# Attention with its weighing in two halves of 256 queries, and its projections in halves of 256 tokens

## The chip, the cores and the metric

The kernel runs on one core of a Trainium2 chip. The core has five engines with queues of their own: TensorE (matrix products, PE in the profile, with PEld for the loading of its weights), VectorE (DVE), ScalarE (ACT), GpSimd (POOL) and SyncE (SP, which issues DMAs here). They meet through semaphores only. The metric is the device time of one execution in microseconds (us); the time of a kernel is the median of its runs.

## The reference

Two layers, each with a norm ahead and behind and a residual: a state-space layer in two directions, and a transformer layer with attention and a mixture of experts. The change touches the attention alone, for 2 sequences of 2048 tokens and 16 heads of 16:

```python
q = (src @ q_w).reshape(b, s, h, hd).transpose(0, 2, 1, 3)
k = (src @ k_w).reshape(b, s, h, hd).transpose(0, 2, 1, 3)
v = (src @ v_w).reshape(b, s, h, hd).transpose(0, 2, 1, 3)
scores = jnp.einsum('bhqd,bhkd->bhqk', q, k) / np.float32(np.sqrt(hd))
scale = jax.nn.sigmoid(jnp.einsum('bhsd,hd->bhs', q, scale_w)) * 2.0
scores = scores * scale[..., None]
aw = jax.nn.softmax(scores, axis=-1)
out = jnp.einsum('bhqk,bhkd->bhqd', aw, v).transpose(0, 2, 1, 3).reshape(b, s, d)
```

## The kernel before

The program has three parts, one behind the other: the state-space layer (to about 670 us), the attention (670 to 2257 us), then gate, routing and experts. The attention works on groups of 4 heads of one sequence (8 groups, `GROUPS`), each in 4 units of 512 queries (`UNITS`, 32 in all), each unit in 16 tiles of 128 keys (`KT`). One tile of a unit is a step here; there are 512.

**A step.** For each of its four heads a step does four things. Two engines share a maximum: TensorE multiplies 128 queries with 512 keys ("max", L1574) and VectorE takes the largest of each row (L1666). This runs `LEAD` = 20 steps ahead of the rest, since a unit's maxima must be complete, negated and put into the query stack before its scores. TensorE multiplies 128 keys with the unit's 512 queries ("score", L1559), the maximum's rows included, so that the difference comes out at once. ScalarE takes the exponential, two heads in one instruction (L1630). TensorE then weighs the values with them ("weigh", L1605) and adds up over the 16 tiles in one PSUM bank, `pv`: the four heads' 17 columns (16 values and a column of ones for the sum) stand side by side in four column groups of the array and run at the same time. The weighing is fp32, so the one matmul of the program is two on the chip, which makes 8 for four heads.

Scores and maxima use 50 and 48 rows of the array: the even heads have the lower half of its rows, the odd heads the upper. A max of an even head and a score of an odd one can run at the same time.

**The order.** `attention_order` writes one list of steps, and each engine does its own part of it in that order. In step t stand max 0, score 1, score 0, max 1, max 2, score 3, score 2, max 3, then the weighing of step t - 1, then what a table `due` plans for this step. The waits that matter here: a max waits until the bank that it writes is free (three banks, `rbank`, in turn, each freed by a reduce or by another reader); score 1 waits for the exp of heads 0 and 1 of the step before, score 3 for that of heads 2 and 3, since they overwrite what it reads; the weighing of a step waits for its two exps; an exp waits for the weighing two steps back, whose input it overwrites.

**What `due` plans.** Once a unit: `negate` (the maxima's sign and split), `turn_rows` (four transposes that make rows of the maxima, a ScalarE copy, DMAs into the query stack) and `turn_out` (four transposes of the weighed sum; the copies L1646 and L1649 and the division around it). Once a group, for the group after it, two batches of `SPLIT`: two projections of 512 tokens to queries and keys (L1081: two matmuls over the depth, four on the chip, then a ScalarE copy, L1101), `scale` (L1091, a Tanh), `multiply` and `high` (L1110, two casts) and `save` (DMAs by SyncE). `SPLIT_AT` gives the steps at which they stand, counted from the batch's first. All of them use the three banks too.

**The first stage.** The first group's projections are in `residual_and_values`, with the residual and the values of the state-space layer's last tokens. The words of `STAGE3` set each engine's order there. Its projections and scales use two banks in turn.

## Time and profile before

| what | value |
|---|---|
| median of 3 runs | 2612.39 us (2609.77 to 2612.70) |
| the profiled execution | 2606.42 us |
| its span, first to last instruction | 2604.6 us |
| TensorE busy | 2455.2 us (94%) |
| VectorE busy | 2103.3 us (81%) |
| ScalarE busy | 1785.0 us (69%) |
| GpSimd busy | 940.3 us (36%) |
| mean granted TensorE clock | 0.972 |

The profile comes from one execution on the chip. A busy time counts an engine's own instructions, not its waits. Matmuls are pipelined, so one that waits for its turn can count as busy: TensorE's 94% does not say that it has no slack. A timeline row merges equal instructions that follow each other (x4): its length then runs from the first one's start to the last one's end. Two rows of TensorE may overlap where they use different halves or columns of the array. The brackets at a row's end give the engine's idle time before it and what ended it. For what a step costs, the distance from one start to the next says more than the lengths. A granted clock of 1.00 is 2.4 GHz, one of 0.50 is 1.2 GHz.

### The profile page before, as it was taken

The numbers are of one execution on the slowest core, as the hardware profiler recorded it, in microseconds if no ns is written. First come the engines' busy times: TensorE is split into PE (matmuls) and PEld (weight loads), VectorE is DVE, ScalarE is ACT, GpSimd is POOL, SyncE is SP. The second block draws the span as 40 slices with busy tenths as digits, with TensorE's granted clock in tenths as the row PEclk, the third lists the DMA queues.
The fourth block names the chain that finished last, engine by engine and source line by source line (L and its number), as shares of the span: only waits on it lengthen the run. The fifth ranks groups of instructions, "written<-read, shape, count | busy, mean of one in ns | idle before, by whom it ended". The sixth has DMA issues, their size and how long they took to land. (4 is left out here: it accounts for less than half of the span.)

```text
span 2604.6 us, 41005 instructions
## 1 busy us (share of the span) xinstructions
PE 2455.2 (94%) x14283; PEld 1173.9 (45%) x14283; DVE 2103.3 (81%) x4155; ACT 1785.0 (69%) x2336; POOL 940.3 (36%) x1059
## 2 busy tenths in 40 slices
PE   7899999999799999999999999999999999897996
PEld 5566655555443333333333333333333333374654
DVE  6778888998768888888888888898899988184886
ACT  4888877777216777777777777777777777862664
POOL 1787888888600112111121121111111010146664
PEclk8999999999878999999999999999999999997998
DMA  3322332232420403104031040040040000125883
GB/s 106 121 82 82 104 95 89 94 108 78 113 55 17 66 18 54 29 18 50 17 47 20 18 63 3 18 66 10 8 66 2 1 2 1 52 90 184 295 288 108
DMA packets 96431, 178.17 MB, mean 68 GB/s; under 512 B 19382, under 2 KB 66150, under 8 KB 88400
## 3 DMA queue, kind: packets, MB, share of 16 engines
q1 hardware_dynamic: 89488, 160.43, 24.4%
q0 software_dynamic: 6016, 14.49, 1.6%
q8 instruction: 114, 1.87, 0.3%
q14 instruction: 93, 0.76, 0.1%
q10 hardware_dynamic: 720, 0.62, 0.1%
HBM read 145.11 MB, written 31.21 MB: 68 GB/s over the span
## 5 line engine op out<-in xcount | busy, mean ns | idle before, releaser
L1666 DVE TENSOR_REDUCE max_part<-round_psum 128x1 f32<-128x512 f32 x2048 | 1271.5, 683 | 220.6 <-PE round_psum L1574 217.4
L1630 ACT ACTIVATE p_exp<-score_psum 128x1024 f32<-128x1024 f32 x1024 | 991.8, 1022 | 287.5 <-PE score_psum L1559 280.0
L1574 PE MATMUL round_psum<-k_stack,q_stack 48*128 48x512 f32 x2048 | 781.2, 459 | 45.7 <-DVE max_part L1666 12.3
L1574 PEld LDWEIGHTS round_psum<-k_stack,q_stack 48*128 48x128 f32 x2048 | 342.4, 186 | 714.0 <-DVE max_part L1666 599.3
L1559 PE MATMUL score_psum<-q_stack,k_stack 50*128 50x512 f32 x2048 | 634.6, 428 | 3.2 <-ACT p_exp L1630 3.2
L1605 PE MATMUL pv_psum<-p_exp,values 128*17 128x512 f32 x4096 | 540.4, 599 | 0.0
L1559 PEld LDWEIGHTS score_psum<-q_stack,k_stack 50*128 50x128 f32 x2048 | 326.2, 185 | 27.3 <-ACT p_exp L1630 23.5
L672 PE MATMUL rot<-tokens_t,w_in 128*128 128x512 f32 x576 | 271.3, 602 | 0.5 <-DVE x_conv L839 0.2
L1709 POOL TENSOR_TENSOR rden<-pv_out,minus_one 128x16 f32<-128x16 f32 x31 | 90.0, 2902 | 439.8 <-ACT pv_out L1649 437.2
L1696 POOL CAST max_parts<-max_neg 128x16 fp32r<-128x16 f32 x32 | 6.4, 199 | 471.6 <-DVE max_neg L1672 451.0
L672 PEld LDWEIGHTS rot<-tokens_t,w_in 128*128 128x128 f32 x576 | 104.3, 193 | 97.5 <-issue 88.1
L930 POOL TENSOR_TENSOR decay<-cum_rows_in,scan_cum 128x1024 f32<-128x1024 f32 x64 | 121.4, 1898 | 55.5 <-DMA cum_rows_in<-cum_rows 34.9
L831 DVE SCALAR_TENSOR_TENSOR rot<-conv_in,chan,rot 128x512 f32<-128x512 f32 x160 | 120.4, 752 | 18.2 <-ACT rot L753 14.6
L723 PE MATMUL rows_psum<-w_out,y_gated 128*128 128x256 f32 x512 | 127.8, 393 | 0.0
L1605 PEld LDWEIGHTS pv_psum<-p_exp,values 128*17 128x17 f32 x4096 | 68.1, 95 | 126.3 <-issue 117.1
L1118 POOL TENSOR_SCALAR split_then_gate<-split_then_gate 128x512 f32<-128x512 f32 x16 | 9.9, 621 | 269.6 <-ACT split_then_gate L1106 269.6
L723 PEld LDWEIGHTS rows_psum<-w_out,y_gated 128*128 128x128 f32 x512 | 93.5, 193 | 10.3
L787 ACT ACTIVATE decay<-decay 128x1024 f32<-128x1024 f32 x64 | 67.4, 1053 | 25.1 <-POOL decay L930 25.1
L1129 POOL TENSOR_TENSOR split_then_gate<-split_then_gate 128x512 f32<-128x512 f32 x32 | 40.3, 1283 | 119.7 <-ACT split_then_gate L1110 119.7
L936 POOL TENSOR_TENSOR c_decayed<-c_decayed,c_t 128x512 f32<-128x512 f32 x60 | 76.8, 1279 | 16.6 <-ACT c_t L772 15.0
L863 DVE TENSOR_TENSOR decay<-decay,gb_psum 128x1024 f32<-128x1024 f32 x64 | 77.9, 1217 | 4.8 <-ACT decay L789 2.2
L693 PE MATMUL y_psum<-decay,x_dt 128*64 128x128 f32 x1024 | 70.9, 281 | 11.3 <-DVE decay L863 8.3
(296 smaller groups left out, 3317.9 us busy)
## 6 DMA issues: line engine op xcount, KB each, us to landing
cum_rows_in<-cum_rows SPq DMA_DIRECT2D x64, 512.0 KB, 3.9
expert_w<-in_expert_w SPq DMA_DIRECT2D x24, 1028.0 KB
qk_rows<-split_then_gate SPq DMA_DIRECT2D x64, 256.0 KB, 4.0
tokens_t<-in_expert_w SPq DMA_DIRECT2D x15, 1028.0 KB, 7.8
cum_pairs_in<-cum_rows SPq DMA_DIRECT2D x240, 64.0 KB, 2.8
q_stack<-qk_rows SPq DMA_DIRECT2D x42, 256.0 KB, 11.7
k_stack<-qk_rows SPq DMA_DIRECT2D x42, 256.0 KB, 15.0
token_rows<-tokens SPq DMA_DIRECT2D x12, 512.0 KB, 4.0
```

Of the source, the lines that this page charges most:

```text
L672: m = nc.tensor.matmul(bank[n, c][:, :], w_in[:, k, col:col + P], xnT[:, k, span(block_at(n) * BLK, BLK, d)], start=(k == 0), stop=(k == K ...
L723: m = nc.tensor.matmul(rows_bank[:, 0:D], yg[:, two, c, :], w_out[d][:, c, :], start=False, stop=(c == CI - 1), skip_group_check=True)
L831: nc.vector.scalar_tensor_tensor(t[:, :], pre[:, c, i:i + BLK], tap(d, c, i), t[:, :], ALU.mult, ALU.add).then_inc(*own.up())
L863: nc.vector.tensor_tensor(mm, mm, over_mid(masked, NH), ALU.mult).then_inc(*m_ready.up(q))
L930: nc.gpsimd.tensor_tensor(heads(M[:, two, :], NH, P), heads(cum[:, q % 2, :], NH, P), over_last(scan_of("cum", d, q), P), ALU.subtract).th ...
L936: nc.gpsimd.tensor_tensor(ceh, ceh, over_mid(CT[:, sl, ch], NH // 2), ALU.mult).then_inc(*c_ready.up(q))
L1559: m = nc.tensor.matmul(ebank[i // 2][:, i % 2, :], ks[rows, n % 2, plane, k * P:(k + 1) * P], qs[rows, n % 2, plane, q * BLK:(q + 1) * BLK ...
L1574: nc.tensor.matmul(bank[step][:, :], qs[rows, n % 2, plane, at:at + P], ks[rows, n % 2, plane, keys * BLK:(keys + 1) * BLK], start=True, s ...
L1605: m = nc.tensor.matmul(pv[h * 32:h * 32 + VW, :], V[:, b * KT + k, g * HG + h, :], pt[:, (k * 2 + h // 2) % 4, h % 2, :], start=(k == 0), ...
L1630: nc.scalar.activation(pt[:, (k * 2 + pair) % 4, :, :], ebank[pair][:, :, :], ACT.Exp).then_inc(*exped.up(u, k, pair))
L1666: nc.vector.tensor_reduce(mx[:, c * HG + h, keys:keys + 1], bank[step][:, :], AX_X, ALU.max).then_inc(*maxed.up(u, k, i))
L1709: nc.gpsimd.tensor_tensor(rden[:, :], o[:, :, HD], minus[:, :].to_broadcast([P, CPB * HG]), ALU.pow).then_inc(*denominator.up(u))
```

## The change

The weighing of a step is cut into two halves of 256 queries each. The first half of step t - 1 stands behind score 3 of step t, the second half behind score 1 of step t + 1, so that two maxima's products lie between one half and the next. All eight matmuls become sixteen on the chip, with the same weights loaded for both halves. Both halves write the same bank; only the first clears it. The exps wait for the second half, and so does the copy of a unit's weighed sum, which now stands one step later on TensorE and is wanted by the next unit's first half in the same step.

The projections of 512 tokens are cut in two as well (256 tokens, half a bank, a copy of half the length each). In the main part they stand at the batch's steps 0, 2, 4 and 6 where they stood at 0 and 4; scale, multiply, high and save keep their steps. In the first stage the second batch's last two quarters stand behind `turn4`, since their banks come free with copies that ScalarE does behind `turn4`.

```diff
-SPLIT = (("project", 0), ("project", 1), ("scale", 0), ("multiply", 0), ("high", 0), ("save", 0))
-SPLIT_AT = (0, 4, 8, 10, 14, 18)
+SPLIT = (("project", 0), ("project", 1), ("project", 2), ("project", 3), ("scale", 0), ("multiply", 0), ("high", 0), ("save", 0))
+SPLIT_AT = (0, 2, 4, 6, 8, 10, 14, 18)
+PART = BLK // 2
...
-        s = 2 * j + i
-        cols = slice(b * SEQ + s * BLK, b * SEQ + (s + 1) * BLK)
+        s, half = 2 * j + i // 2, i % 2
+        first = b * SEQ + s * BLK + half * PART
+        cols = slice(first, first + PART)
...
-            m = nc.tensor.matmul(bank[:, :], S.w_qk[:, k, g, i * w:(i + 2) * w], S.srcT[:, k, cols], start=(k == 0),
-                                 stop=(k == KD - 1))
-        m.then_inc(*S.projected.up(n, s))
+            m = nc.tensor.matmul(bank[:, 0:PART], S.w_qk[:, k, g, i // 2 * w:(i // 2 + 2) * w], S.srcT[:, k, cols],
+                                 start=(k == 0), stop=(k == KD - 1))
+        m.then_inc(*S.projected.up(n, s, half))
...
-        nc.scalar.copy(S.parts[:, i, 1, :], bank[:, :]).then_inc(*S.raw_in.up(n, s))
+        nc.scalar.copy(S.parts[:, i // 2, 1, half * PART:(half + 1) * PART],
+                       bank[:, 0:PART]).then_inc(*S.raw_in.up(n, s, half))
...
-    "PE": "project00 project01 scale0 project10 project11 values0 values1 turn4 scale1 values2 values3 turn5 "
+    "PE": "project00 project01 project02 project03 scale0 project10 project11 values0 values1 turn4 project12 project13 "
+          "scale1 values2 values3 turn5 "
...
-        if weighing:
-            yield "weigh", *divmod(t - 1, KT), 0
+            if left == ("max", 0) and 0 <= t - 2 < total:
+                yield "weigh", *divmod(t - 2, KT), 1
+            if left == ("max", 2) and 0 <= t - 1 < total:
+                yield "weigh", *divmod(t - 1, KT), 0
...
-                    if k == 0 and u:
+                    if k == 0 and i == 0 and u:
                         pe.wait_ge(*pv_out.at(u - 1))
+                    part = slice(i * PART, (i + 1) * PART)
                     for h in range(HG):
-                        if h % 2 == 0:
+                        if h % 2 == 0 and i == 0:
                             pe.wait_ge(*exped.at(u, k, h // 2))
-                        m = nc.tensor.matmul(pv[h * 32:h * 32 + VW, :], V[:, b * KT + k, g * HG + h, :],
-                                             pt[:, (k * 2 + h // 2) % 4, h % 2, :], start=(k == 0), stop=(k == KT - 1),
-                                             skip_group_check=True)
-                        if h % 2:
+                        m = nc.tensor.matmul(pv[h * 32:h * 32 + VW, part], V[:, b * KT + k, g * HG + h, :],
+                                             pt[:, (k * 2 + h // 2) % 4, h % 2, part], start=(k == 0 and i == 0),
+                                             stop=(k == KT - 1), skip_group_check=True)
+                        if h % 2 and i:
                             m.then_inc(*weighed.up(u, k, h // 2))
...
-                if what == "weigh" and k == KT - 1:
+                if what == "weigh" and k == KT - 1 and i:
```

In the order of TensorE a plain step stood like this before (L1574 a max, L1559 a score, L1605 the weighing of four heads; "x2" are two instructions in a row; the first row is a step's first max):

```order
L1574 MATMUL round_psum1<-k_stack,q_stack 128x512
L1559 MATMUL score_psum0<-q_stack,k_stack 128x512 x2
L1574 MATMUL round_psum2<-k_stack,q_stack 128x512
L1574 MATMUL round_psum0<-k_stack,q_stack 128x512
L1559 MATMUL score_psum1<-q_stack,k_stack 128x512 x2
L1574 MATMUL round_psum1<-k_stack,q_stack 128x512
L1605 MATMUL pv_psum<-p_exp,values 17x512 x4
```

And like this now (L1581 a max, L1566 a score, L1613 half a weighing), again from a step's first max to the next step's:

```order
L1581 MATMUL round_psum0<-k_stack,q_stack 128x512
L1566 MATMUL score_psum0<-q_stack,k_stack 128x512
L1613 MATMUL pv_psum<-p_exp,values 17x256 x4
L1566 MATMUL score_psum0<-q_stack,k_stack 128x512
L1581 MATMUL round_psum1<-k_stack,q_stack 128x512
L1581 MATMUL round_psum2<-k_stack,q_stack 128x512
L1566 MATMUL score_psum1<-q_stack,k_stack 128x512
L1613 MATMUL pv_psum<-p_exp,values 17x256 x4
L1566 MATMUL score_psum1<-q_stack,k_stack 128x512
L1581 MATMUL round_psum0<-k_stack,q_stack 128x512
L1581 MATMUL round_psum1<-k_stack,q_stack 128x512
```

The weighing of 512 queries at the step's end is gone; half of one stands between score 1 and score 0, which write the same bank pair, and half of one between score 3 and score 2.

A projection stood between a weighing and the next step's first max on TensorE (L1081; the row says x2 for the depth's two halves):

```order
L1574 MATMUL round_psum1<-k_stack,q_stack 128x512
L1605 MATMUL pv_psum<-p_exp,values 17x512 x4
L1081 MATMUL round_psum2<-tokens_t,split_then_gate 128x512 x2
L1574 MATMUL round_psum0<-k_stack,q_stack 128x512
L1559 MATMUL score_psum0<-q_stack,k_stack 128x512 x2
```

Now a half of one (L1084) stands between a step's last max and the next step's first:

```order
L1613 MATMUL pv_psum<-p_exp,values 17x256 x4
L1566 MATMUL score_psum1<-q_stack,k_stack 128x512
L1581 MATMUL round_psum2<-k_stack,q_stack 128x512
L1084 MATMUL round_psum0<-tokens_t,split_then_gate 128x256 x2
L1581 MATMUL round_psum1<-k_stack,q_stack 128x512
L1566 MATMUL score_psum0<-q_stack,k_stack 128x512
```

It is no longer behind a weighing, it writes 256 columns instead of 512, and there are twice as many such places.

ScalarE's copies of the projections (L1101 before, L1104 now) lie between the exps (L1630, L1638). Before, at one batch:

```order
L1101 COPY split_then_gate<-round_psum 128x512
L1630 ACTIVATE p_exp<-score_psum 128x1024 x8
L1101 COPY split_then_gate<-round_psum 128x512
L1641 COPY max_rows<-round_psum 8x512
L1630 ACTIVATE p_exp<-score_psum 128x1024 x6
L1646 COPY pv_out<-pv_psum 128x512
L1630 ACTIVATE p_exp<-score_psum 128x1024 x2
```

And now, the end of the same batch:

```order
L1638 ACTIVATE p_exp<-score_psum 128x1024 x4
L1104 COPY split_then_gate<-round_psum 128x256
L1649 COPY max_rows<-round_psum 8x512
L1638 ACTIVATE p_exp<-score_psum 128x1024 x4
L1104 COPY split_then_gate<-round_psum 128x256
L1638 ACTIVATE p_exp<-score_psum 128x1024 x2
L1654 COPY pv_out<-pv_psum 128x512
L1638 ACTIVATE p_exp<-score_psum 128x1024 x2
```

The copy of the weighed sum (L1646, now L1654) keeps its place among the exps; the projections' copies are half as long, and four exps apart instead of eight.

## Rows read from the trace of the kernel before

**Rows 1.** Busy time by window: each engine's us (x instructions), clock, DMA share, GB/s.
```profile
770.00:795.00 25.00, 23.93 (x65) 11.86 (x65) 16.62 (x28) 7.20 (x11) 2.92 (x4) 0.50 0.17 44
795.00:2200.00 1405.00, 1368.18 (x8161) 513.09 (x8157) 1211.33 (x1971) 1027.46 (x1126) 204.83 (x275) 1.00 0.17 27
```

**Rows 2.** Groups by line, 795 to 2212 us: count | busy us, mean ns | idle before, releaser.
```profile
L1666 DVE TENSOR_REDUCE max_part<-round_psum 128x1 f32<-128x512 f32 x1959 | 1216.3, 683 | 195.1 <-PE round_psum L1574 192.1
L1630 ACT ACTIVATE p_exp<-score_psum 128x1024 f32<-128x1024 f32 x980 | 949.9, 1022 | 280.7 <-PE score_psum L1559 273.2
...
L1605 PE MATMUL pv_psum<-p_exp,values 128*17 128x512 f32 x3920 | 515.8, 598 | 0.0
...
L1081 PE MATMUL round_psum<-tokens_t,split_then_gate 128*128 128x512 f32 x104 | 51.6, 618 | 0.0
...
L1614 PE MATMUL round_psum<-const_f,pv_out 128*128 128x128 f32 x120 | 19.7, 287 | 0.0
L1593 PE MATMUL round_psum<-const_f,max_parts 128*8 128x128 f32 x120 | 18.0, 273 | 0.0
L1646 ACT COPY pv_out<-pv_psum 128x512 f32<-128x512 f32 x30 | 17.6, 588 | 4.2 <-PE pv_psum L1605 0.3
...
L1110 ACT CAST split_then_gate<-split_then_gate 128x512 fp32r<-128x512 f32 x26 | 14.8, 627 | 0.0
```

**Rows 3.** Timeline of one plain step: start us, length us, instruction, [idle before <-releaser].
```profile
2021.70 0.50 PE L1574 MATMUL round_psum<-k_stack,q_stack 48*128 48x512 f32 x1
...
2022.04 0.39 PE L1574 MATMUL round_psum<-k_stack,q_stack 48*128 48x512 f32 x1
...
2022.24 2.48 DVE L1666 TENSOR_REDUCE max_part<-round_psum 128x1 f32<-128x512 f32 x4 [0.22 <-PE round_psum L1574]
2022.28 0.40 PE L1574 MATMUL round_psum<-k_stack,q_stack 48*128 48x512 f32 x1
2022.47 1.94 ACT L1630 ACTIVATE p_exp<-score_psum 128x1024 f32<-128x1024 f32 x2 [0.77 <-PE score_psum L1559]
...
2022.98 0.18 PEld L1574 LDWEIGHTS round_psum<-k_stack,q_stack 48*128 48x128 f32 x1 [0.52 <-DVE max_part L1666]
2022.98 0.50 PE L1574 MATMUL round_psum<-k_stack,q_stack 48*128 48x512 f32 x1
...
2023.41 1.05 PE L1605 MATMUL pv_psum<-p_exp,values 128*17 128x512 f32 x8
...
2024.39 0.49 PE L1574 MATMUL round_psum<-k_stack,q_stack 48*128 48x512 f32 x1
...
2024.39 0.73 PE L1559 MATMUL score_psum<-q_stack,k_stack 50*128 50x512 f32 x2
```

**Rows 4.** Timeline, TensorE: four matmuls of 256 columns, and four of 512 (a projection).
```profile
756.26 1.13 PE L1585 MATMUL score_psum<-w_v,tokens_t 128*128 128x256 f32 x4
757.33 0.50 PE L1574 MATMUL round_psum<-k_stack,q_stack 48*128 48x512 f32 x2
...
900.28 1.98 PE L1081 MATMUL round_psum<-tokens_t,split_then_gate 128*128 128x512 f32 x4
...
902.20 0.50 PE L1574 MATMUL round_psum<-k_stack,q_stack 48*128 48x512 f32 x1
```

**Rows 5.** Timeline of the last steps, which have no maxima.
```profile
2212.39 0.73 PE L1559 MATMUL score_psum<-q_stack,k_stack 50*128 50x512 f32 x4
...
2212.94 3.77 ACT L1630 ACTIVATE p_exp<-score_psum 128x1024 f32<-128x1024 f32 x4 [0.53 <-PE score_psum L1559]
...
2214.93 0.19 PEld L1559 LDWEIGHTS score_psum<-q_stack,k_stack 50*128 50x128 f32 x2 [0.70 <-ACT p_exp L1630]
...
2251.78 0.92 PE L1559 MATMUL score_psum<-q_stack,k_stack 50*128 50x512 f32 x4
```

**Rows 6.** Timeline, TensorE, from the first stage's last turns to the first max.
```profile
712.72 1.80 PE L1295 MATMUL score_psum<-const_f,p_exp 128*128 128x128 f32 x8 [0.61 <-DVE p_exp L1337]
...
717.43 1.19 PE L1574 MATMUL round_psum<-k_stack,q_stack 48*128 48x512 f32 x3 [2.91 <-DMA k_stack<-qk_rows]
```

More of the change, by code:

```diff
@@ L1046, in __init__ @@
         self.filled = sems.dma("rows_fill", self.fills)
-        self.projected = sems.events("qk_projected", blocks)
+        parts = [(n, s, half) for n, s in blocks for half in range(2)]
+        self.projected = sems.events("qk_projected", parts)
         self.scaled = sems.events("qk_scale_summed", halves)
-        self.raw_in = sems.events("qk_raw_stored", blocks)
+        self.raw_in = sems.events("qk_raw_stored", parts)
         self.ez_in = sems.events("qk_scale_exp", halves)
@@ L1073, in split_on_tensor @@
     if what == "project":
-        s = 2 * j + i
-        cols = slice(b * SEQ + s * BLK, b * SEQ + (s + 1) * BLK)
-        if (n, s) in ((0, 0), (1, 0)):
+        s, half = 2 * j + i // 2, i % 2
+        first = b * SEQ + s * BLK + half * PART
+        cols = slice(first, first + PART)
+        if (n, s, half) in ((0, 0, 0), (1, 0, 0)):
             pe.wait_ge(*S.loaded[n].at(0))
@@ L1089, in split_on_tensor @@
         for s, x, _, q in S.blocks(j):
-            pe.wait_ge(*S.raw_in.at(n, s))
+            pe.wait_ge(*S.raw_in.at(n, s, 1))
             m = nc.tensor.matmul(bank[q, :], S.w_sc[q, g, :], x[q, :], start=True, stop=True, skip_group_check=True)
@@ L1096, in split_on_scalar @@
     if what == "project":
-        s = 2 * j + i
-        act.wait_ge(*S.projected.at(n, s))
-        if (n, j) != (0, 0):
+        s, half = 2 * j + i // 2, i % 2
+        act.wait_ge(*S.projected.at(n, s, half))
+        if (n, j) != (0, 0) and half == 0:
             act.wait_ge(*(S.saved[s - 2].at(n, "k") if j else S.saved[s + 2].at(n - 1, "k")))
-        nc.scalar.copy(S.parts[:, i, 1, :], bank[:, :]).then_inc(*S.raw_in.up(n, s))
+        nc.scalar.copy(S.parts[:, i // 2, 1, half * PART:(half + 1) * PART],
+                       bank[:, 0:PART]).then_inc(*S.raw_in.up(n, s, half))
     if what == "scale":
@@ L1165 @@
     "SP": "weights0 load4 load7 weights1 load6 load5 keep4 keep5 save0 fill stack0 keep6 save1 keep7",
-    "PE": "project00 project01 scale0 project10 project11 values0 values1 turn4 scale1 values2 values3 turn5 "
+    "PE": "project00 project01 project02 project03 scale0 project10 project11 values0 values1 turn4 project12 project13 "
+          "scale1 values2 values3 turn5 "
           "turn6 turn7",
-    "ACT": "project00 project01 scale0 high0 values0 values1 turn4 project10 project11 scale1 values2 high1 "
+    "ACT": "project00 project01 project02 project03 scale0 high0 values0 values1 turn4 project10 project11 project12 project13 scale1 values2 high1 "
            "turn5 turn6 turn7 values3",
@@ L1219, in bank_read @@
         what, n, j, i = u
-        return S.raw_in.at(n, 2 * j + i) if what == "project" else S.ez_in.at(n, j)
+        return S.raw_in.at(n, 2 * j + i // 2, i % 2) if what == "project" else S.ez_in.at(n, j)
     x_load = [sems.dma(f"x_again{b}", [b]) for b in later]
@@ L1418, in attention_order @@
     for t in range(-LEAD, total + 4):
-        scoring, weighing, ahead = 0 <= t < total, 0 < t <= total, 0 <= t + LEAD < total
+        scoring, ahead = 0 <= t < total, 0 <= t + LEAD < total
         u, k = divmod(t, KT)
@@ L1505, in bank_read @@
             return out_in.at(n)
-        return S.raw_in.at(n, 2 * j + i) if what == "project" else S.ez_in.at(n, j)
+        return S.raw_in.at(n, 2 * j + i // 2, i % 2) if what == "project" else S.ez_in.at(n, j)
     def back(u, k, n):
@@ L1543, in _ @@
             pe.wait_ge(*zero.at(0))
-            pe.wait_ge(*S.raw_in.at(0, SB - 1))
+            pe.wait_ge(*S.raw_in.at(0, SB - 1, 1))
             pe.wait_ge(*S.ez_in.at(0, 1))
```

## The prediction

> **What bounds the kernel now.** I read the windows first: from 795 to 2200 us, more than half of the span, TensorE is busy 1368 of 1405 us at the full granted clock of 1.00 (2.4 GHz), VectorE 1211, ScalarE 1027 [rows 1]. All of the change's main part lies there. Then the groups of lines, for the size of one of each [rows 2], and one plain step in order of time [rows 3]. A step is one tile of 128 keys for one unit: four maxima's products ("max", L1574), four score products (L1559), two exps, one weighing (L1605).
>
> In [rows 3] the step runs from the max at 2021.70 to the next one's at 2024.39: 2.69 us. The reader is to see one closed circle in it. The first max starts at 2021.70; VectorE begins to reduce it at 2022.24 (0.54 later); the fourth max needs the bank that this reduce gives back and starts at 2022.98 (0.74 later, its weights' load idle for 0.52 "<-DVE max_part"); the weighing starts 0.43 later, and the next step's first max 0.98 after that. 0.54 + 0.74 + 0.43 + 0.98 = 2.69. VectorE itself needs only 2.40: four reduces take 2.48 from first start to last end, one is 0.68 long, so one starts every 0.60. ScalarE needs 1.84: two exps take 1.94, one 1.02, so one starts every 0.92. So neither TensorE's work nor VectorE's is the limit, but their turn-taking: four maxima come in a bunch, then none while TensorE weighs.
>
> **The weighing in halves.** Three prices from [rows 3], counted from start to start. A product that finds its weights loaded ahead takes 0.40, one that stands first after another shape of work 0.50. From such a first pair to the next pair it is 0.34 (2021.70 to 2022.04), later 0.24. A weighing starts 0.07 before the last product ends (2022.98 + 0.50 against 2023.41), so 0.43 after the start of a first one and 0.33 after the start of one with its weights ahead.
>
> The trace has no weighing of 256 queries. A full one holds TensorE 0.98. What 256 columns less are worth is read from the projections [rows 4]: four matmuls of 512 columns hold it 1.92 (900.28 to 902.20), four of 256 columns 1.07 (756.26 to 757.33), so 0.2125 for one. The weighing's four heads run side by side, in two rounds: 490 weighings of 8 matmuls are busy 515.8 us, 1.05 each, though one matmul lasts 0.598 [rows 2]. A half then holds TensorE 0.98 - 2 x 0.2125 = 0.555. Below, everything could halve: 0.49. Above, by the group of 256 columns, which loads 128 weight columns instead of 17, two of its four matmuls less: 1.07 - 0.425 = 0.645. I take 0.555, which comes from the weighing's own row; the ends go into the range.
>
> The new step has three bounds.
> TensorE's own work: first pair and half a weighing behind it (0.43 + 0.555), first pair again and a pair with weights ahead (0.34 + 0.33), second half (0.555), first pair (0.34): 2.55.
> VectorE: 2.40. The fourth max now comes 2.21 after the first, its bank is free after 1.28, so the wait of today is gone.
> A new circle through ScalarE: score 1 waits for the exp of the step before (that wait stands today too, with 0.9 us to spare: the exp that starts at 2022.47 is over at 2023.49 and the score starts at 2024.39). From now on half a weighing stands between score 1 and score 0, and score 0 is what the next exp wants. Score 1 to half weighing 0.43, half weighing 0.555, score 0 and up to the exp's start 0.50 + 0.04 (2022.04 + 0.40 to 2022.47), exp 1.02, and 0.05 from its end to the next score 1: in [rows 5] the second exp of the row at 2212.94 starts 0.92 later and ends at 2214.88, and the weights' load that waited for it starts at 2214.93. Sum 2.595. Queued behind that waiting score are the half weighing, the next maxima and all else of TensorE.
> The longest is the new circle: **2.595 against 2.69**, 0.095 less a step. That is what the change gains, a third of what VectorE alone would allow. There are 492 steps with maxima: 492 x 0.095 = **-46.7 us**.
>
> **The steps without maxima.** The last 20 steps have none. Today they go at ScalarE's pace: from 2212.39 to 2251.78 are 19 steps, 2.07 each [rows 5]. The new circle has no max in it, so it holds there too: 20 x (2.595 - 2.07) = **+10.5**.
>
> **The projections.** Counts of the main part from [rows 2]: 104 matmuls are 26 projections, at 1.92 more each: 49.9 us. They become 52. One stands between the last pair (which then costs 0.43 instead of 0.34) and the next step, and takes 1.07: the step is 2.55 + 0.09 + 1.07 = 3.71, 1.115 above 2.595; together 58.0, **+8.1**. The ScalarE copies are half as long and fit beside; a bank is held for a shorter time. SyncE's and GpSimd's queues keep their steps: scale, multiply, high and save stand at the same steps as before.
>
> **Other work that meets the new circle.** 30 turns of the maxima's rows and 30 of the output (120 matmuls in fours of each kind): today each adds its own length, in future its length + 0.09 - 0.045 (2.595 is 0.045 above TensorE's 2.55): 60 x 0.045 = **+2.7**. 13 pairs of casts (L1110, 26 of 0.627): two hold ScalarE about 1.05. The second exp starts 1.225 after the first (0.34 + 0.33 + 0.555) and is on for 0.92, so ScalarE has 2.595 - 1.225 - 0.92 = 0.45 free before the next first exp: 0.60 late each time. Today the free stretch is 0.77 (2022.47 in [rows 3]), 0.28 late: 13 x 0.32 = **+4.2**. The 30 copies of the weighed sum (L1646, 0.588, some 0.49 to the next start): 0.04 over the free 0.45, and the next unit's first half weighing now waits for them within the same step: 0.05 each, **+1.5**.
>
> **The start.** Two of the first batch's quarter projections move behind turn 4 on TensorE, and the scale, the values and the last turns are queued behind them, at a clock that is low in places (0.50 from 770 to 795, [rows 1]): 2 to 4 us later. TensorE is 2.9 us idle before the first max, which waits for k_stack's DMA at 717.43, and is done with the turns at 714.5 [rows 6]. That hides most: **+1** (0 to 2).
>
> **Sum:** -46.7 + 10.5 + 8.1 + 2.7 + 4.2 + 1.5 + 1 = **-18.7 us**. The profiled execution took 2606.42 (span 2604.6 and 1.8 around it): 2587.7. The median of the three runs is 6.0 above it; the same step off 2612.39 gives **2594 us**.
>
> **Rivals.** Faster still: a half weighing is nearer to 0.49. The circle is then 2.53 and TensorE 2.42: 492 x 0.16 = 78.7 off, the others as above (+17.5) with 9.2 instead of 10.5 for the last steps: -52, **2560**. For it: the weighing's weights are 17 columns wide, little to load. Against: each change of shape costs the same drain however short the work.
>
> Slower: the half weighing is not nearly half. At 0.645 TensorE itself is the bound, 2.55 + 0.18 = 2.73: 492 x 0.04 = +20, last steps +12.3 (the circle is 2.685), projections 58.5 + 1 - 49.9 = +9.6, turns 60 x 0.09 = +5.4, the rest +6.7: **+54, 2666**. It decides from where the step's gain no longer pays the 28 us of the other terms: 28 / 492 = 0.057, a step of 2.633, a half weighing of 0.59. For it: the one group of 256 columns that the trace has lies above that. Against: its weights are the wide ones.
> The Trainium skill speaks for this one ("TensorEngine Tiling (Array Packing)", section "Instruction Overhead"): each matmul has about 60 cycles of overhead on TRN2. The step gets eight matmuls more; at 2.4 GHz that is, as an estimate, 0.2 us a step and a half weighing of 0.655, about as in this rival. The trace speaks against it so far: eight matmuls of 0.598 within 1.05 [rows 2] do not queue for their overhead one by one.
>
> No change: the gain is there, but ScalarE's small works do not fit into its free stretches, which are now two, of 0.3 and 0.45, where there was one. If the 30 copies of the weighed sum fall on the circle in full, 0.49 each instead of 0.05, it is +13.2: **2607**, and a half weighing 0.01 longer makes it 2612. For it: ScalarE is in the circle, as it isn't today. Against: the copies stand where the longer stretch is.
>
> **How the numbers follow.** The forecast (half weighing 0.51 to 0.58): 0.50. Faster still: 0.14. No change: 0.18. Slower: 0.18. What a measurement of this kernel can tell from no change is about 0.2%, 5 us. The forecast's and the faster rival's chances make faster 0.64. The range leaves out the deeper half of the fast rival and the deeper half of the slow one: a half weighing of 0.51 (circle 2.55) gives -41, one of 0.60 (TensorE 2.64) +7: 2572 to 2620. TensorE's clock in the lead (0.50 in [rows 1]) may fall at other places, some us either way, within it.
>
> **What would show it.** In the profile after: a plain step of 2.58 to 2.61; ahead of score 1 an idle stretch that ends with an exp, and none any more that ends with a reduce ahead of the fourth max; a half weighing that holds TensorE 0.55; VectorE and ScalarE with more busy share there; the last 20 steps near 2.6 instead of 2.07; a quarter projection at 1.07. If the plain step is 2.69 or more with TensorE never idle, the half weighing was mis-sized; if it is under 2.55, the circle through ScalarE was.

## The result and the profile after

The changed kernel takes 2596.88 us (median of 15 runs, 2583.94 to 2611.38), the kernel before 2611.74 (median of 15 runs beside it). The ratio is 0.9942, with a 95% interval of 0.9924 to 0.996: 14.9 us faster, 0.6%. Predicted were 2594 and 18.7 us less. The profiled executions differ by 16.4 us: a span of 2588.2 after, 2604.6 before. Of all executions below, one of adjacent's ten took 3029.64 us at a mean granted clock of 0.721; it counts in adjacent's median, but in no ratio.

Where these 16.4 us lie is read from the starts of the first max, of the first exp, of the first exp of step 491 (the last one with maxima) and of step 511 (the last one):

| stretch | before, us | after, us | difference | predicted |
|---|---|---|---|---|
| up to the first max | 717.4 | 717.2 | -0.2 | +1 |
| first max to first exp (the lead) | 70.9 | 67.8 | -3.2 | 0, some us either way |
| first exp to step 491 | 1422.1 | 1392.3 | -29.8 | -30.2 |
| the last 20 steps | 41.9 | 53.2 | +11.4 | +10.5 |
| the rest (last turn, gate, experts) | 352.3 | 357.7 | +5.4 | 0 |
| span | 2604.6 | 2588.2 | -16.4 | -18.7 |

The -30.2 are the prediction's steps, projections, turns, casts and copies together. The two stretches that the change touches in earnest came out within 1 us of the prediction each. The lead, with two of the projections in it, and the rest, which the change doesn't touch, are taken up in the last section.

The windows of the kernel after that answer to [rows 1] (time, then each engine's busy time and instructions, the granted clock, DMA share, GB/s):

```profile
770.00:795.00 25.00, 24.29 (x99) 11.16 (x98) 18.01 (x31) 9.56 (x13) 2.49 (x2) 0.57 0.16 43
795.00:2176.00 1381.00, 1376.30 (x12196) 599.46 (x12192) 1242.53 (x1981) 1079.07 (x1157) 204.82 (x275) 1.00 0.17 28
```

In the main part TensorE leaves 4.7 us free where it left 37. VectorE's share is 90.0% (86.2% before), ScalarE's 78.1% (73.1%): the same work in less time. TensorE looks like the bound. That it isn't can't be read from this sum, but from the order within one step and from an experiment, both below: by the profile's own note the matmuls' ends are modelled, and a wait of some 0.05 us ahead of one hardly shows in such a sum.

The groups by line of the kernel after, 795 to 2178 us, for [rows 2] (count | busy us, mean ns | idle before, releaser):

```profile
L1674 DVE TENSOR_REDUCE max_part<-round_psum 128x1 f32<-128x512 f32 x1954 | 1239.1, 687 | 137.6 <-PE round_psum L1581 109.1
L1638 ACT ACTIVATE p_exp<-score_psum 128x1024 f32<-128x1024 f32 x977 | 999.7, 1025 | 295.2 <-PE score_psum L1566 295.2
...
L1613 PE MATMUL pv_psum<-p_exp,values 128*17 128x256 f32 x7812 | 611.6, 385 | 1.9
...
L1581 PEld LDWEIGHTS round_psum<-k_stack,q_stack 48*128 48x128 f32 x1953 | 296.6, 184 | 39.8 <-DVE max_part L1674 30.1 <-issue 9.4 <-ACT pv_out L1657 0.2
...
L1084 PE MATMUL round_psum<-tokens_t,split_then_gate 128*128 128x256 f32 x208 | 58.8, 405 | 0.0
```

And of the kernel before, the group that loads the weights of the maxima's products, 795 to 2212 us:

```profile
L1574 PEld LDWEIGHTS round_psum<-k_stack,q_stack 48*128 48x128 f32 x1957 | 325.2, 184 | 679.6 <-DVE max_part L1666 576.0 <-issue 28.5 <-ACT pv_out L1649 13.4
```

The wait that the change was to remove is gone: the idle time of these loads that ends with a reduce fell from 576.0 us to 30.1, and none of what is left stands ahead of a fourth max. The 576.0 are not all that wait, though. By the max that a load is for, 230.6 of them stand ahead of a fourth max (490 loads, 0.52 in [rows 3]) and 345.5 ahead of a step's first (426 loads), most of these behind a weighing, like this one:

```profile
2024.39 0.18 PEld L1574 LDWEIGHTS round_psum<-k_stack,q_stack 48*128 48x128 f32 x1 [0.85 <-DVE max_part L1666]
```

There only the loading of weights is idle; TensorE is busy with the weighing (2023.41 to 2024.46, [rows 3]) and loses nothing by it. So the change could gain far less than these 576 us; the steps with maxima became 29.8 us shorter. The weighing's matmuls are twice as many (7812) and their busy time grew from 515.8 to 611.6.

One plain step of the kernel after, in order of time (start, length, instruction, [idle before and what ended it]), for [rows 3]:

```profile
2034.24 0.50 PE L1566 MATMUL score_psum<-q_stack,k_stack 50*128 50x512 f32 x1
...
2034.66 0.63 PE L1613 MATMUL pv_psum<-p_exp,values 128*17 128x256 f32 x8
...
2035.22 0.49 PE L1566 MATMUL score_psum<-q_stack,k_stack 50*128 50x512 f32 x1
...
2035.56 0.40 PE L1566 MATMUL score_psum<-q_stack,k_stack 50*128 50x512 f32 x1
2035.75 1.02 ACT L1638 ACTIVATE p_exp<-score_psum 128x1024 f32<-128x1024 f32 x1 [0.34 <-PE score_psum L1566]
...
2035.89 0.63 PE L1613 MATMUL pv_psum<-p_exp,values 128*17 128x256 f32 x8
...
2036.44 0.50 PE L1566 MATMUL score_psum<-q_stack,k_stack 50*128 50x512 f32 x1
...
2036.83 0.50 PE L1566 MATMUL score_psum<-q_stack,k_stack 50*128 50x512 f32 x1
```

This is the new circle. Score 1 starts at 2034.24, the half weighing 0.42 later, score 0 another 0.56 later (2035.22), the exp that wants score 0 at 2035.75 (0.53); the exp lasts 1.02, to 2036.77; the next step's score 1 starts 0.06 after that, at 2036.83. 0.42 + 0.56 + 0.53 + 1.02 + 0.06 = 2.59. The step is 2.59 long.

The last steps of the kernel after, which have no maxima, for [rows 5]:

```profile
2179.36 0.74 PE L1566 MATMUL score_psum<-q_stack,k_stack 50*128 50x512 f32 x2
...
2179.89 1.02 ACT L1638 ACTIVATE p_exp<-score_psum 128x1024 f32<-128x1024 f32 x1 [0.34 <-PE score_psum L1566]
...
2180.97 0.18 PEld L1566 LDWEIGHTS score_psum<-q_stack,k_stack 50*128 50x128 f32 x1 [0.21 <-ACT p_exp L1638]
...
2182.49 1.02 ACT L1638 ACTIVATE p_exp<-score_psum 128x1024 f32<-128x1024 f32 x1 [0.35 <-PE score_psum L1566]
```

From exp to exp it is 2182.49 - 2179.89 = 2.60, as in the steps with maxima, and not 2.07 as before. Here, where no max stands beside it, the profile names the wait: the weights' load of score 1 sat idle until the exp ended (2179.89 + 1.02 = 2180.91, load at 2180.97). This is the clearest single line for the circle.

### The profile page after: what moved, and what is told of

Read it like the earlier page. It is cut to its first block and busy times, and to the rows that moved or that the text cites. A ratio compares the mean times of both kernels' runs of the same rounds, so it can differ in the third digit from the quotient of the medians.

```text
span 2588.2 us, 49485 instructions
## 1 busy us (share of the span) xinstructions
PE 2467.5 (95%) x18507; PEld 1267.0 (49%) x18507; DVE 2129.0 (82%) x4155; ACT 1836.0 (71%) x2368; POOL 940.4 (36%) x1059
## 5 line engine op out<-in xcount | busy, mean ns | idle before, releaser
L1674 DVE TENSOR_REDUCE max_part<-round_psum 128x1 f32<-128x512 f32 x2048 | 1297.8, 687 | 161.6 <-PE round_psum L1581 132.8
L1638 ACT ACTIVATE p_exp<-score_psum 128x1024 f32<-128x1024 f32 x1024 | 1047.3, 1025 | 313.3 <-PE score_psum L1566 313.3
L1566 PE MATMUL score_psum<-q_stack,k_stack 50*128 50x512 f32 x2048 | 843.5, 474 | 4.7 <-ACT p_exp L1638 2.8
L1581 PE MATMUL round_psum<-k_stack,q_stack 48*128 48x512 f32 x2048 | 787.3, 461 | 8.5 <-DVE max_part L1674 4.9
L1613 PE MATMUL pv_psum<-p_exp,values 128*17 128x256 f32 x8192 | 642.3, 385 | 2.3 <-ACT pv_out L1654 0.3
L1566 PEld LDWEIGHTS score_psum<-q_stack,k_stack 50*128 50x128 f32 x2048 | 363.5, 184 | 478.8 <-issue 434.0
L1581 PEld LDWEIGHTS round_psum<-k_stack,q_stack 48*128 48x128 f32 x2048 | 313.9, 187 | 71.2 <-DVE max_part L1674 52.6
L1613 PEld LDWEIGHTS pv_psum<-p_exp,values 128*17 128x17 f32 x8192 | 136.0, 95 | 271.5 <-issue 257.5
L1084 PE MATMUL round_psum<-tokens_t,split_then_gate 128*128 128x256 f32 x256 | 75.2, 422 | 7.0 <-DMA split_then_gate<-in_w_qk 6.0
```

Of the source, the lines that this page charges most:

```text
L1566: m = nc.tensor.matmul(ebank[i // 2][:, i % 2, :], ks[rows, n % 2, plane, k * P:(k + 1) * P], qs[rows, n % 2, plane, q * BLK:(q + 1) * BLK ...
L1581: nc.tensor.matmul(bank[step][:, :], qs[rows, n % 2, plane, at:at + P], ks[rows, n % 2, plane, keys * BLK:(keys + 1) * BLK], start=True, s ...
L1613: m = nc.tensor.matmul(pv[h * 32:h * 32 + VW, part], V[:, b * KT + k, g * HG + h, :], pt[:, (k * 2 + h // 2) % 4, h % 2, part], start=(k = ...
L1638: nc.scalar.activation(pt[:, (k * 2 + pair) % 4, :, :], ebank[pair][:, :, :], ACT.Exp).then_inc(*exped.up(u, k, pair))
L1674: nc.vector.tensor_reduce(mx[:, c * HG + h, keys:keys + 1], bank[step][:, :], AX_X, ALU.max).then_inc(*maxed.up(u, k, i))
```

## The experiments

Two theories of the changed kernel's step stand against each other. By the first, the step is the circle through ScalarE, and cutting a weighing costs next to nothing. By the second, TensorE is the bound: it is busy 1376.30 of 1381 us, since eight more matmuls a step cost it what the removed wait gave. All seven runs, beside the two of above; the ratio is against runs of the kernel before beside them (medians 2610.15 for adjacent, weigh_only, project_only and short_exp, 2609.97 for the last three). "Plain step" is the median of the steps with nothing else in them:

| kernel | median, us | ratio (95%) | plain step | first exp to step 491 | last 20 steps |
|---|---|---|---|---|---|
| before | 2611.74 | | 2.69 | 1422.1 | 41.9 |
| changed | 2596.88 | 0.9942 (0.9924 to 0.996) | 2.59 | 1392.3 | 53.2 |
| adjacent | 2614.62 | 1.0015 (1.0005 to 1.0024) | 2.69 | 1424.6 | 41.9 |
| weigh_only | 2591.23 | 0.9931 (0.9913 to 0.9948) | 2.59 | 1388.4 | 53.2 |
| project_only | 2615.45 | 1.0025 (1.001 to 1.0039) | 2.69 | 1426.0 | 41.8 |
| short_exp | 2527.91 | 0.9677 (0.9662 to 0.9693) | 2.44 | 1341.5 | 45.6 |
| pairs_apart | 2515.71 | 0.9635 (0.9621 to 0.9649) | 2.44 | 1324.6 | 44.5 |
| pairs_apart_h | 2521.87 | 0.9656 (0.962 to 0.9692) | 2.44 | 1324.8 | 44.5 |
| changed_again | 2598.91 | 0.9949 (0.9929 to 0.997) | 2.59 | 1393.1 | 53.2 |

**adjacent: what does the cut itself cost?** The kernel before, with the weighing cut into the change's two halves, but both left where the whole one stood.

```
         if weighing:
             yield "weigh", *divmod(t - 1, KT), 0
+            yield "weigh", *divmod(t - 1, KT), 1
...
-                        m = nc.tensor.matmul(pv[h * 32:h * 32 + VW, :], V[:, b * KT + k, g * HG + h, :],
+                        m = nc.tensor.matmul(pv[h * 32:h * 32 + VW, part], V[:, b * KT + k, g * HG + h, :],
...
```

> The kernel before with each weighing cut into its two halves of 256 queries, but both halves left where the whole one stood, at the step's end, one behind the other; projections whole. It prices the cut alone. Theory (a half holds TensorE 0.555 because the change of shape ahead and behind is the fixed part, and the cut itself costs next to nothing): two halves side by side pay one change of shape, so they hold 0.98 to 1.01; a plain step of 2.69 to 2.72, 2612 to 2627 us. Rival (each set of matmuls has its own fixed part of 0.13): the two hold 1.11, a plain step of 2.82, 492 x 0.13 = 64 more, about 2676 us.

Measured: 2614.62, ratio 1.0015. The timeline of one step, TensorE:

```profile
2030.36 0.49 PE L1576 MATMUL round_psum<-k_stack,q_stack 48*128 48x512 f32 x1
...
2031.63 0.18 PEld L1576 LDWEIGHTS round_psum<-k_stack,q_stack 48*128 48x128 f32 x1 [0.52 <-DVE max_part L1669]
...
2032.06 1.06 PE L1608 MATMUL pv_psum<-p_exp,values 128*17 128x256 f32 x16
...
2033.05 0.49 PE L1576 MATMUL round_psum<-k_stack,q_stack 48*128 48x512 f32 x1
```

The 16 matmuls of both halves hold TensorE 2033.05 - 2032.06 = 0.99, where 8 of twice the length held it 0.98 [rows 3]; the step is 2.69 as before, with the old wait for a reduce (0.52) in it. So the eight matmuls more cost 0.01 us a step: the price of more matmuls, on which the slower rival and the second theory lean, isn't there. Whether halves that stand apart fill TensorE all the same, short_exp decides. The Trainium skill ("TensorEngine Tiling (Array Packing)", section "Instruction Overhead") gives each matmul an overhead of about 60 cycles; for eight that would be, as an estimate, 0.2 us. Four heads side by side on 32 columns each do not pay it one after the other here. The section can also be read as a least length (it says that one column takes as long as 60); a matmul of 256 columns would then pay nothing more, and the 0.01 agrees with that.

What a half costs when it stands apart is a second thing: 0.56 twice is 1.12, against 0.98. This 0.14 is what it costs that other products stand between the halves, one more change of shape, and it is in the prediction's 0.555.

**weigh_only and project_only: each half of the change alone.** The first has the halves of the weighing where the change puts them, and whole projections; the second the other way round.

```
# weigh_only, against the changed kernel
-SPLIT_AT = (0, 2, 4, 6, 8, 10, 14, 18)
+SPLIT_AT = (0, 4, 8, 10, 14, 18)
...
-            m = nc.tensor.matmul(bank[:, 0:PART], S.w_qk[:, k, g, i // 2 * w:(i // 2 + 2) * w], S.srcT[:, k, cols],
-                                 start=(k == 0), stop=(k == KD - 1))
+            m = nc.tensor.matmul(bank[:, :], S.w_qk[:, k, g, i * w:(i + 2) * w], S.srcT[:, k, cols], start=(k == 0),
+                                 stop=(k == KD - 1))
...
```

```
# project_only, against the changed kernel
-            if left == ("max", 0) and 0 <= t - 2 < total:
-                yield "weigh", *divmod(t - 2, KT), 1
-            if left == ("max", 2) and 0 <= t - 1 < total:
-                yield "weigh", *divmod(t - 1, KT), 0
+        if weighing:
+            yield "weigh", *divmod(t - 1, KT), 0
...
```

> The change without its second part: the weighing's halves two maxima's products apart, the projections whole as before. Theory: plain steps of 2.59 as in the changed kernel, last steps 2.6; a whole projection makes a step of 2.55 + 0.09 + 1.92 = 4.56, 1.97 over a plain one, 26 x 1.97 = 51 against 58 for 52 halves: 7 us less than the changed kernel, near 2590. Rival (halves of projections pay because VectorE and ScalarE run on meanwhile): 5 us or more above the changed kernel, 2602 or more.

> The change without its first part: whole weighings at the step's end as before, projections in halves, in the first stage too. Theory: plain steps of 2.69; a half projection adds 1.07 where a whole one adds 1.92, 52 x 1.07 - 26 x 1.92 = 5.7 more, about 2617 us. Rival (the halves of the projections carry part of the change's gain): 2607 or less.

Measured: 2591.23 and 2615.45. The weighing brings the whole gain. The projections' cut costs 3.9 us from the first exp to step 491 on either footing: 1392.3 against 1388.4 with the halves of the weighing, 1426.0 against 1422.1 without. In the median of the runs the cut alone is slower by little (ratio 1.0025, from 1.001 on). Between weigh_only and the changed kernel the medians differ by 5.7, but the intervals of their ratios overlap: the run times alone don't separate the two. (The cut has a second effect, in the lead; the last section has it.)

**short_exp: is it the circle through ScalarE?** The changed kernel, with each exp over 256 of its 512 columns a head; it leaves out the other 256, so the second half weighing reads what was left there.

```
-                    nc.scalar.activation(pt[:, (k * 2 + pair) % 4, :, :], ebank[pair][:, :, :],
+                    nc.scalar.activation(pt[:, (k * 2 + pair) % 4, :, 0:PART], ebank[pair][:, :, 0:PART],
```

> The changed kernel with each exp over half of its columns (two heads x 256 instead of 512), so the weighing's second half reads what was left there; TensorE's and VectorE's work is the same. It shortens only the circle score 1, half weighing, score 0, exp. Theory (that circle sets the 2.59): exp 0.59 instead of 1.02, circle 2.16, so TensorE is the bound with all weights loaded ahead, 0.33 + 0.555 + 0.34 + 0.33 + 0.555 + 0.34 = 2.45; plain steps of 2.45, 492 x 0.14 = 69 less, and about 8 less in the last 20 steps: near 2520 us. Rival (TensorE's own work is 2.59): plain steps stay at 2.59, only the last steps shorten, 2587 to 2597 us.

Measured: 2527.91, ratio 0.9677. One step:

```profile
1991.19 0.50 PE L1566 MATMUL score_psum<-q_stack,k_stack 50*128 50x512 f32 x1
...
1991.53 0.40 PE L1566 MATMUL score_psum<-q_stack,k_stack 50*128 50x512 f32 x1
...
1991.73 0.60 ACT L1638 ACTIVATE p_exp<-score_psum 128x512 f32<-128x512 f32 x1 [0.63 <-PE score_psum L1566]
1991.86 0.63 PE L1613 MATMUL pv_psum<-p_exp,values 128*17 128x256 f32 x8
...
1992.41 0.49 PE L1566 MATMUL score_psum<-q_stack,k_stack 50*128 50x512 f32 x1
...
1993.09 0.63 PE L1613 MATMUL pv_psum<-p_exp,values 128*17 128x256 f32 x8
...
1993.64 0.49 PE L1566 MATMUL score_psum<-q_stack,k_stack 50*128 50x512 f32 x1
```

TensorE has the same instructions as in the changed kernel, and the step falls from 2.59 to 1993.64 - 1991.19 = 2.45. An engine that is the bound doesn't get faster by another engine's shorter work, so TensorE wasn't: the circle was. 2.45 is then TensorE's own work, twice 0.34 + 0.33 + 0.555. The last 20 steps, too, lose 7.6 us. The whole is 8 us above what I expected: I had taken 0.14 off all 492 steps (69 us), and the steps with maxima lost 50.8 (1392.3 to 1341.5). The steps with a projection, a turn or a scale lost nothing (3.706 us with a projection in both), so TensorE held them already. The 340 plain ones lost 0.121 each on the mean (41 us), the 13 with casts 0.435 and the 23 with a copy of the weighed sum 0.165 (together 9.5). Their mean, 2.477, lies above their median of 2.45 since the first ones ran at a lower clock: from 784 to 800 us it was 0.50 on the mean, in the changed kernel 0.77.

**pairs_apart and pairs_apart_h: can the circle be opened, with the computation whole?** The half weighings move: away from between score 1 and score 0, to behind the pairs (score 0, max 1) and (score 2, max 3), one pair earlier. The first has whole projections, the second halved ones as in the change.

```
-            if left == ("max", 0) and 0 <= t - 2 < total:
-                yield "weigh", *divmod(t - 2, KT), 1
-            if left == ("max", 2) and 0 <= t - 1 < total:
-                yield "weigh", *divmod(t - 1, KT), 0
+            if left == ("score", 0) and 0 <= t - 1 < total:
+                yield "weigh", *divmod(t - 1, KT), 0
+            if left == ("score", 2) and 0 <= t - 1 < total:
+                yield "weigh", *divmod(t - 1, KT), 1
...
```

> The weighing in halves, both at other places: half 0 behind the step's second pair (score 0, max 1), half 1 behind its last (score 2, max 3), both of the step before; projections whole. Two maxima still lie between two halves, but no half stands between score 1 and score 0 any more: score 0 follows in 0.34, its exp is over 1.85 after score 1 began, 0.6 to spare. Theory: TensorE is the bound, 2 x (0.34 + 0.33 + 0.555) = 2.45, near VectorE's 2.40; 492 x 0.24 = 118 less than before; last steps near 2.1 as before; the copy of a unit's sum now holds up the next unit's first half by about half a us, 30 x 0.5 = 15, and casts and turns some us more: 2505 to 2520 us. Rival (any half weighing costs the step what it cost in the change, wherever it stands): plain steps near 2.59, 2590 us.

> The same order of the weighing with the projections in halves as in the change. Theory: as project_only and weigh_only showed, halves cost 4 to 8 us more than whole ones: plain steps of 2.45, 2510 to 2527 us, above pairs_apart. Rival (with VectorE near its own limit the shorter stops of the maxima pay): at or below pairs_apart.

Measured: 2515.71 and 2521.87, ratios 0.9635 and 0.9656. One step of pairs_apart, and its main part as a window:

```profile
2029.69 0.50 PE L1577 MATMUL round_psum<-k_stack,q_stack 48*128 48x512 f32 x1
...
2030.03 0.39 PE L1577 MATMUL round_psum<-k_stack,q_stack 48*128 48x512 f32 x1
...
2030.35 0.63 PE L1609 MATMUL pv_psum<-p_exp,values 128*17 128x256 f32 x8
2030.46 1.02 ACT L1634 ACTIVATE p_exp<-score_psum 128x1024 f32<-128x1024 f32 x1 [0.20 <-PE score_psum L1562]
...
2030.91 0.50 PE L1577 MATMUL round_psum<-k_stack,q_stack 48*128 48x512 f32 x1
...
2031.58 0.63 PE L1609 MATMUL pv_psum<-p_exp,values 128*17 128x256 f32 x8
...
2032.14 0.50 PE L1577 MATMUL round_psum<-k_stack,q_stack 48*128 48x512 f32 x1
```

```profile
795.00:2110.00 1315.00, 1305.10 (x12106) 477.31 (x12106) 1206.78 (x1981) 1077.21 (x1131) 204.64 (x275) 1.00 0.18 29
```

Two half steps of 1.22 and 1.23 (2029.69, 2030.91, 2032.14): 2.45, with the exp at its full 1.02. That is the step that short_exp needed half an exp for. Score 0 and the exp behind it no longer have a weighing ahead of them, so ScalarE starts its exps evenly, 1.22 apart: the exp of 2030.46 is over at 2031.48, 0.66 before the product that wants its bank starts (2032.14). The last 20 steps cost 2.6 more than before, not 11.4. This version beats both kernels: by the medians 94 us under the kernel before (2609.97 beside it) and 83 under the changed one (2598.91 beside it). Whether the projections are whole or halved makes no difference there that these runs can tell (first exp to step 491: 1324.6 and 1324.8; the intervals of the ratios overlap).

**changed_again: the changed kernel beside these.**

> The changed kernel as it is, beside the two others on the same chip. Both theories: near 2597 us, plain steps of 2.59.

Measured: 2598.91, ratio 0.9949 (0.9929 to 0.997), as in the first comparison.

## Why the prediction was right, step by step

**The step.** 2.595 was predicted and 2.59 measured, and not by luck of the sum: its five parts, 0.43, 0.555, 0.54, 1.02 and 0.05, measured 0.42, 0.56, 0.53, 1.02 and 0.06. That it is the circle, and not merely as long as it, short_exp shows (2.45 with a shorter exp), the last steps show (2.60 without any max), and pairs_apart shows (2.45 once the weighing is out of the circle).

**The steps with something else in them.** The 491 steps sorted by what stands in them, each from the start of its first exp to that of the next step, mean us:

| in the step | before | after |
|---|---|---|
| nothing else | 2.699 (360) | 2.598 (340) |
| turn of the output | 3.270 (29) | 3.220 (24) |
| turn of the maxima's rows | 3.215 (26) | 3.172 (26) |
| copy of the weighed sum | 2.683 (24) | 2.706 (23) |
| the casts | 2.855 (13) | 3.182 (13) |
| scale | 3.695 (11) | 3.655 (11) |
| projection alone | 4.625 (17) | 3.706 (37) |

The remaining steps have two of these. Each row's excess over a plain step, after less before, gives the terms:

- Plain step: 0.101 x 491 = -49.6, where -46.7 was predicted.
- Projections, 1.926 over a plain step before (26) and 1.108 after (52; nine of them, which share their step with a turn, only some 0.95): about 56.2 against 49.6, +6.6 for the predicted +8.1. The step of 3.71 was right (3.706): behind a projection score 1 does stand first after another shape, as the 2.55 in that sum has it.
- Turns: 0.571 became 0.622 and 0.516 became 0.574, 60 x 0.054 = +3.2 for +2.7.
- Casts: 0.156 became 0.584, 13 x 0.43 = +5.6 for +4.2. The 0.60 of after was right, the 0.28 of before was less.
- Copies of the weighed sum: from 0.016 under a plain step to 0.108 over it, 30 x 0.124 = +3.7 for +1.5.
- Scales, which the prediction left out: 0.996 became 1.057, 13 x 0.06 = +0.8.

Together -29.7, as measured (-29.8). That the sum came within 0.5 us of the -30.2 is in part luck: the plain steps and the projections gave 4.4 us more than predicted, and turns, casts, copies and scales cost 4.9 more. So with the whole: the lead gave 3.2 and the rest took 5.4, and both stood at nothing in the sum.

**The last 20 steps**: +11.4 for +10.5. **The start**: -0.2 for +1. The scale behind the moved projections ran 2.3 us later (700.45 instead of 698.16), within the 2 to 4 predicted; but by the last eight turns, which wait for other engines, nothing was left of it: they start at 712.49 (before 712.72) and end at 713.55 (714.52). The first max waited for k_stack's DMA in both, 3.67 us instead of 2.91 [rows 6].

**The bounds that didn't decide.** One was wrong: TensorE's own work, predicted at 2.55, is 2.45. I had counted score 1 as a pair without its weights loaded ahead (0.43), which it is only because it waits for the exp; released in time it costs 0.33, as short_exp shows (1991.53 to 1991.86). Since the circle was the longer, the forecast didn't suffer. The slower rival's price did: with a half weighing of 0.645 TensorE would have been at 2.63 and the circle at 2.685, so its step was 0.05 too long; and by its own terms its projections come to +10.4 (52 x 1.16 - 49.9) and not +9.6.

**The rivals.** Faster still needed a half near 0.49: it is 0.56. Slower needed 0.59 or more; adjacent shows that the number of matmuls costs 0.01. No change needed ScalarE's copies on the circle in full, 0.49 each: they cost 0.12, more than the 0.05 of the forecast.

**What was to be seen.** The plain step, the half of 0.55, the absent wait for a reduce and the last steps all are there. One mark was not: an idle stretch ahead of score 1 that ends with an exp. The wait is so short (0.06 from the exp's end to the product, with another product still ending on TensorE) that in the plain steps the profile mostly shows no idle time for it, only in the last steps. A circle in which each link waits a little for the last need not show as one engine's idle time.

## What to carry to other kernels

When a long piece of work on an in-order queue is cut to shorten one wait, follow each engine's circle through the new places: here the cut alone was nearly free (0.01 us a step, and 0.14 once the halves stand apart), but the place put half a weighing between a product and the exp that the next product waits for, and more than half of the gain stayed there (0.10 us a step came out where pairs_apart gives 0.24). Put the pieces behind the product that another engine is waiting for, not ahead of it: the same pieces moved by one pair gave 2521.87 (pairs_apart_h) where the change gave 2598.91 beside it. And a busy share near 100% (1376.30 of 1381 us) doesn't make an engine the bound; shortening another engine's work tells.

## What was not expected of the hardware

**The clock in the lead.** The halved projections gain 3.2 us in the lead, where two of them stand. Over the nine profiles the lead takes 70.9 to 71.1 in the four kernels with whole projections, 67.8 in four of the five with halved ones, and 64.4 in the fifth (short_exp). The windows of the lead, before and after (columns as above, the granted clock third from the end):

```profile
717.40:788.40 71.00, 65.43 (x166) 32.03 (x166) 50.22 (x82) 9.38 (x23) 6.08 (x7) 0.69 0.28 56
```

```profile
717.20:785.00 67.80, 62.90 (x174) 32.27 (x174) 50.41 (x82) 9.69 (x25) 6.07 (x7) 0.73 0.28 60
```

The clock is 0.69 and 0.73 on the mean (1.00 is 2.4 GHz, 0.50 is 1.2; there is nothing between in these profiles). In the kernel before it is low from 712.9 to 730.0, 736.8 to 747.0 and from 767.6 on, in the changed one from 716.2 to 729.9 and from 760.5 on. Within the lead that is 43.6 us against 37.0: what takes 6.6 us at the low level takes 3.3 at the high one, and the lead is 3.2 shorter. A part of the lead, 735 to 750 us, of before, after, weigh_only and project_only, in this order:

```profile
735.00:750.00 15.00, 14.06 (x33) 6.39 (x32) 8.59 (x15) 2.08 (x5) 0.00 (x0) 0.66 0.00 0
```

```profile
735.00:750.00 15.00, 13.89 (x52) 7.62 (x51) 12.54 (x20) 2.61 (x7) 0.00 (x0) 1.00 0.00 1
```

```profile
735.00:750.00 15.00, 14.17 (x33) 6.86 (x33) 8.79 (x15) 1.70 (x4) 0.00 (x0) 0.66 0.00 0
```

```profile
735.00:750.00 15.00, 13.84 (x50) 7.45 (x49) 12.06 (x20) 2.98 (x8) 0.00 (x0) 1.00 0.00 1
```

With halved projections the clock is 1.00 in these 15 us, with whole ones 0.66, and VectorE, which reduces what TensorE delivers, is busy 12.54 and 12.06 us instead of 8.59 and 8.79; TensorE is busy about as long in all four. Behind it, from 750 to 790 us, the halved ones give some of that back (before, then after):

```profile
750.00:790.00 40.00, 36.15 (x101) 18.65 (x102) 30.32 (x51) 7.40 (x16) 6.08 (x7) 0.72 0.10 27
```

```profile
750.00:790.00 40.00, 36.99 (x105) 18.29 (x104) 28.35 (x47) 8.78 (x17) 6.07 (x7) 0.63 0.10 27
```

So the -3.2 belongs to the projections' part of the change, and fits what the clock gives. That the clock alone moves the lead, short_exp shows: up to the first exp its program is that of the changed kernel, it has 26.9 us at the low level there instead of 37.0, and its lead takes 64.4 instead of 67.8. Why the clock holds at 2.4 GHz from 735 to 750 us with the one and not with the other was not tried.

**The rest.** It takes 352.3 to 360.3 over the nine profiles, and no edit touches it. Its windows of before and after:

```profile
2252.20:2604.00 351.80, 302.83 (x1369) 197.55 (x1367) 243.73 (x850) 192.35 (x437) 188.88 (x182) 0.93 0.57 184
```

```profile
2230.50:2588.00 357.50, 302.69 (x1384) 196.56 (x1382) 243.65 (x850) 192.11 (x437) 189.13 (x182) 0.92 0.56 181
```

The busy times of all five engines agree within 1 us, and the stretch is 5.7 us longer. The granted clock goes with its length: over the nine profiles it is 0.926 where the rest is shortest (before) and 0.907 to 0.910 in the three of 357.5 to 360.3 us (pairs_apart, pairs_apart_h, weigh_only). A straight line through the nine rises by 0.46 us for each us at the low level; the changed kernel has 7.7 us more of it there than the kernel before (59.6 against 51.9), which by that line is some 3.5 of the 5.4. What moves the clock there, no run settles.

**The spread.** The runs of one kernel differ, and the granted clock goes with them: the 15 runs of the changed kernel lie between 2583.94 us at a mean clock of 0.975 and 2611.38 at 0.962, the eight of changed_again between 2583.98 (0.975) and 2603.0 (0.966). pairs_apart_h (2503.1 to 2528.62) and project_only (2606.72 to 2626.99) spread as far, pairs_apart (2508.3 to 2518.81) and the kernel before beside project_only (2605.28 to 2614.51) less. But weigh_only, with whole projections, goes from 2585.01 to 2599.96, short_exp, with halved ones, from 2519.43 to 2530.91, and the kernel before from 2602.44 to 2619.44 beside the changed one: that halved projections make the spread is not shown.

The profiled executions of the changed kernel (2590.0 and 2589.71), project_only (2611.41) and pairs_apart_h (2515.7) each lie below the median of their kernel, so none of their longer runs has a trace, and where the clock falls in those stays open. By the profiled spans the projections' cut is worth -3.2 in the lead and +3.9 behind it (+0.2 in pairs_apart_h), next to nothing; by the medians the three kernels with it lie 5 to 8 us above the same kernel without it. That difference is measured in one of the three pairs (project_only, ratio 1.0025), and its cause is not shown.
